# Two routed scatters: GpSimd's wait moved from every eighth transfer's own landing to every fourth, for the four before

## The reference, cut to what matters

```python
logits = flat.astype(jnp.float32) @ router_w.T + router_bias
scores = jax.nn.softmax(logits, axis=-1)
topk_scores, topk_idx = jax.lax.top_k(scores, TOPK)
topk_scores = topk_scores / jnp.clip(topk_scores.sum(axis=-1, keepdims=True), 1e-12, None)
h = jax.nn.silu(jnp.einsum('nd,ehd->neh', flat, gate_w)) * jnp.einsum('nd,ehd->neh', flat, up_w)
expert_out = jnp.einsum('neh,edh->ned', h, down_w)
sel = jnp.take_along_axis(expert_out, topk_idx[:, :, None], axis=1)
out = (sel * topk_scores.astype(flat.dtype)[:, :, None]).sum(axis=1)
out = out + jax.nn.silu(flat @ sgate_w.T) * (flat @ sup_w.T) @ sdown_w.T
```

## Time and profile before

| | |
|---|---|
| median of 3 runs | 1180.38 us (1178.22 to 1186.05) |
| profiled execution | 1180.22 us, of it a span of 1178.4 us |
| granted TensorE clock, mean | 0.837 of full speed |
| busy: PE, DVE, ACT, POOL | 859.4, 738.5, 660.3, 514.8 us |
| layer 0's routed stage | about 305 to 643 us |
| layer 1's routed stage | about 886 us to the end |

### The profile page before, as it was taken

One profiled execution on the slowest core, in us unless ns is written; L12 is line 12 of the kernel. 1 busy time (PEld: TensorE's weight loads), 2 busy tenths in 40 slices (PEclk: granted clock), 3 DMA queues, 4 the chain that ended last, 5 costly groups with the idle time before them and its releaser, 6 DMA issues. The chain is left out here.

```text
span 1178.4 us, 19964 instructions
## 1 busy us (share of the span) xinstructions
PE 859.4 (73%) x5812; PEld 698.0 (59%) x5812; DVE 738.5 (63%) x2343; ACT 660.3 (56%) x1352; POOL 514.8 (44%) x634
## 2 busy tenths in 40 slices
PE   3796666666156999995996546787676999999900
PEld 2633455555145888995995223444345989999900
DVE  5579588888765466410668599997986551004636
ACT  4354777777453324663664657677675656666600
POOL 0002555555206666666774777000002666125365
PEclk9998677777555999997998767788885999999965
DMA  7960000000511115655774111000004123233232
GB/s 207 290 195 0 1 0 0 0 0 1 222 34 43 46 43 159 188 165 154 192 195 128 48 45 48 0 1 1 1 1 165 42 90 105 86 84 102 60 91 60
DMA packets 133844, 97.00 MB, mean 82 GB/s; under 512 B 11648, under 2 KB 125696, under 8 KB 132736
## 3 DMA queue, kind: packets, MB, share of 16 engines
q1 hardware_dynamic: 121472, 70.79, 20.0%
q0 software_dynamic: 12288, 25.19, 7.3%
HBM read 45.61 MB, written 50.33 MB: 81 GB/s over the span
## 5 line engine op out<-in xcount | busy, mean ns | idle before, releaser
L1117 POOL DMA_INDIRECT e_xs<-h_tok,rows_of x128 | 129.3, 1010 | 101.2 <-DVEq L1600 35.4
L735 ACT ACTIVATE mask<-ps_q,k_neg 128x256 bf16<-128x256 f32 x256 | 101.0, 489 | 35.1 <-PE ps_q L850 35.1
L1130 POOL DMA_INDIRECT e_got<-e_ys,e_rows_of x64 | 65.9, 1030 | 93.7 <-DMA e_ys<-e_y_rows 67.9
L850 PE MATMUL ps_q<-q_parts,pick 128*128 (+1 forms) x256 | 59.1, 366 | 49.7 <-DVE mask L651 42.1
L1266 PE MATMUL e_ps_gu<-e_w_all,e_x_turned 128*128 x384 | 92.7, 385 | 0.5 <-ACT e_x_turned L1435 0.5
L1758 DVE TENSOR_TENSOR e_hidden<-e_ps_gu,e_hidden 128x512 f32<-128x512 f32 x48 | 33.2, 691 | 93.9 <-ACT e_hidden L1441 93.6
L1117 POOL DMA_INDIRECT e_xs<-h_tok,e_rows_of x64 | 65.5, 1023 | 51.3 <-DVEq L1600 19.2
L1298 PE MATMUL e_ps_up<-e_x_turned,e_w_up 128*128 128x128 f32 x640 | 84.5, 275 | 1.0 <-ACT e_x_turned L1435 1.0
L2253 POOL DMA_INDIRECT c_got<-e_ys,rows_of x64 | 71.1, 1111 | 31.3 <-issue 19.2
L1309 PE MATMUL e_ps_y<-e_w_all,e_hidden 128*128 x640 | 84.2, 275 | 0.0
L651 DVE TENSOR_TENSOR mask<-ps_q,k_tok 128x1024 bf16<-128x1024 f32 x64 | 75.2, 1216 | 10.2 <-PE ps_q L850 8.2
(11 more groups left out here) (399 smaller groups left out, 2430.9 us busy)
## 6 DMA issues: line engine op xcount, KB each, us to landing
e_x_rows<-e_xs SPq DMA_DIRECT2D x68, 256.0 KB, 2.9
e_ys<-e_y_rows SPq DMA_DIRECT2D x68, 256.0 KB, 2.5
e_xs<-zeros SPq DMA_DIRECT2D x2, 6144.0 KB, 34.2
e_w_all<-in_w SPq DMA_DIRECT2D x4, 1536.0 KB, 13.0
e_xs<-zeros SPq DMA_DIRECT2D x2, 2560.0 KB, 27.8
e_w_all<-in_w SPq DMA_DIRECT2D x4, 1024.0 KB, 10.2
x_tok<-in_x SPq DMA_DIRECT2D x4, 512.0 KB, 6.0
e_xs<-h_tok,rows_of POOLq DMA_INDIRECT x128, 2.3
```

Source lines behind the costliest of these rows:

```text
L735: last = nc.scalar.activation(mask[u][QS // 2 + j][keys][:, h * T:(h + 1) * T], psq[1][:, h * T:(h + 1) * T], ACT.Sign, bias=k_neg[u][:, k ...
L850: last = nc.tensor.matmul(psq[0 if on_dve else 1][:, h * T:(h + 1) * T], pick[:, (quad * HQ + h) * P:(quad * HQ + h + 1) * P], q_parts[:, ...
L1117: nc.gpsimd.indirect_dma_start(out=xs[part], out_offset=bass.IndirectOffsetOnAxis(ap=rows_of[:, t * K + k:t * K + k + 1], axis=0), in_=til ...
L1130: nc.gpsimd.indirect_dma_start(out=got[t % GB][:, k * P:(k + 1) * P], out_offset=None, in_=ys[part], in_offset=bass.IndirectOffsetOnAxis(a ...
```

## The change

The wait for landings moves back by four transfers and comes after every fourth. Each part has two semaphores in place of one for each group of four tiles; fours of transfers raise them in turn. After a four, GpSimd waits for the four before it, not for the one just issued. The last four of a part is waited for by SP's first load alone. SP waits for both semaphores of the part to reach their whole count. The same lines serve both layers.

```diff
-        scattered = [plain(f"scattered{i}") for i in range(GROUPS)]
+        CHUNK = 4
+        CHUNKS = PT * K // CHUNK
+        scattered = [[plain(f"scattered{part}_{i}") for i in range(2)] for part in range(NP)]
...
                     if q == 0:
-                        for g in range(part * GPP, (part + 1) * GPP):
-                            sp.wait_ge(scattered[g], 16 * TPG * K)
+                        for done in scattered[part]:
+                            sp.wait_ge(done, 16 * CHUNK * CHUNKS // 2)
...
                             nc.gpsimd.indirect_dma_start(
                                 out=xs[part], out_offset=bass.IndirectOffsetOnAxis(ap=rows_of[:, t * K + k:t * K + k + 1], axis=0),
-                                in_=tile(h_tok, t), in_offset=None, bounds_check=ROWS - 1).then_inc(scattered[t // TPG], 16)
-                        if (t + 1) * K % 8 == 0:
-                            pool.wait_ge(scattered[t // TPG], 16 * K * (t % TPG + 1))
+                                in_=tile(h_tok, t), in_offset=None,
+                                bounds_check=ROWS - 1).then_inc(scattered[part][(t - part * PT) * K // CHUNK % 2], 16)
+                        c, rest = divmod((t - part * PT + 1) * K, CHUNK)
+                        if rest == 0 and c >= 2:
+                            pool.wait_ge(scattered[part][c % 2], 16 * CHUNK * (c // 2))
```

## The result

| | before | after |
|---|---|---|
| median | 1180.88 us (1178.22 to 1186.05, 6 runs) | 1173.17 us (1170.36 to 1174.46, 6 runs) |
| profiled execution | 1180.22 us, span 1178.4 | 1170.36 us, span 1168.6 |

The ratio is 0.9926, with a 95% interval of 0.9908 to 0.9944: between 6.6 and 10.9 us less. The forecast of 1172.8 lies 0.4 us from the median. The profiled execution of after is the fastest of its six runs, so not all of its 9.8 us may be put down to the change; which part may is told behind the rows. One execution of an experiment's kernel ("layer 1 alone") was in a slow state, 1311.3 us at a granted clock of 0.688, and is left out of its median.

A forecast was written before the change was run, and what follows sets the result against it. The scatter was taken to bound only the seam between layer 0's halves. The gathers allowed 6.1 + 1.3 = 7.4 us, TensorE 8.2; the later end decides, layer 1 counts nothing: 1180.2 - 7.4 = 1172.8 us, range 1168.5 to 1178.0.

The forecast's parts named there:

- The drains and the waits: Layer 0's scatter: 16 drains removed, 30 waits cost nothing unless a landing passes 5.7 us; part 1 ends 18.8 us early.
- TensorE's path: Seam of layer 0's halves: load 24 follows the last store, so TensorE restarts at 541.7, 8.2 us sooner.
- no gain of clock: TensorE at the seam: the shorter stand still slows its clock; were it kept up, 2.4 us more.
- GpSimd's path: Layer 0: first gather waits for part 0's stores, starts 6.1 us sooner; with 1.3 slack, 7.4 us, which decides.
- The step took 3.3: Seam: from part 0's last store issued to the first gather, layer 1's 3.2 us plus 0.1.
- the 1.3 of slack: Layer 0's end: the last gathers landed 1.3 us before VectorE combined them; range 0.1 to 1.6.
- VectorE's wait of 0.8: Layer 0's end: VectorE waits some 0.8 us for the last gathers.
- The stages behind: After layer 0: everything between the layers moves as a whole; layer 1 loses 13.2 us of drains, costed at nothing.
- B: Layer 0: more slack in the gathers and TensorE keeps its clock, 10.6 us gained, 1169.6; chance 0.08.
- C: Scatter: transfers take longer on GpSimd without drains; gain gone at about 27 us more, 1180; chance 0.10.
- D: Scatter: undrained transfers pile up and land later, 14.2 us late at a landing of 8.0, 1194.4; chance 0.06.

The follow-up runs named there:

- layer 1 alone: Against the kernel before: new wait only in layer 1, layer 0 left instruction for instruction; 1180.70 us beside 1180.28, ratio 1.0002.
- one behind: Changed kernel with fours made ones: behind every transfer GpSimd waits for the one before it; 1201.88 us, ratio to before 1.0167.
- two behind: Changed kernel with fours made twos: behind every second transfer a wait for the two before; 1171.49 us, ratio to before 0.993.
- eight behind: Changed kernel with fours made eights: GpSimd waits for the eight before; 1173.61 us beside 1180.28, ratio to before 0.9942.
- drains on two semaphores: Changed kernel with the new wait in layer 1 only; layer 0 drains behind every eighth, each drain over two semaphores; 1183.86 us, ratio to before 1.0037.
- the changed kernel again: The changed kernel, nothing altered, measured once more beside other kernels; 1172.23 us, ratio to before 0.993.
- part 0 alone: Changed kernel with the new wait only in part 0 of layer 0, drains behind every eighth elsewhere; 1172.3 us, ratio to before 0.9938.

## Why the prediction was right

**The drains and the waits.** Forecast: waits behind four cost nothing, part 1 starts at 435.1 and its last transfer at 517.8. Found: 434.81 and 517.99, and every gap within a part 0.30 to 0.32. The kernels with one, two and eight behind confirm the step that the wait holds only where a landing passes its cover: in nearly every pair with one behind, at a few with two (where none was forecast), never with four or eight.

**TensorE's path.** Forecast: load 24 at 539.0, restart at 541.7, a stand of 3.9, no gain of clock. The times on the clock lie 1.3 to 1.8 earlier, since this execution's first turn did (450.99 against 452.75). Counted from that turn the restart is 7.8 us sooner, not 8.2. The load took 540.37 - 537.20 = 3.17 us to TensorE where 2.64 was taken over from before. The clock did fall, as assumed, but the row it was read from was weaker than it looked; more on that at the end.

**GpSimd's path** decides, as forecast, and here lies the term that was mis-sized. The last store was issued at 526.85 + 10.23 - 0.36 = 536.72 and the first gather started at 540.43, 3.71 later. The step took 3.3, from layer 1, where it was 3.20 before and is 3.20 after (1039.03 to 1042.23). The last store landed in 2.8 us at the seam, and in 2.3 in layer 1: the whole 0.5 by which this step is longer than layer 1's, and inside the 2.3 to 3.6 that the forecast allowed for. A stretch view of after shows what differs around it; first the seam, then layer 1 (length, busy time of the five engines, clock, DMA share, GB/s):

```profile
536.70:540.40 3.70, 0.03 (x1) 0.03 (x1) 0.00 (x0) 0.00 (x0) 0.00 (x0) 0.83 0.96 269
1039.00:1042.20 3.20, 3.20 (x31) 3.20 (x30) 0.00 (x0) 2.23 (x4) 0.00 (x0) 1.00 0.47 136
```

At the seam four loads are issued right behind the last store, and the DMA engines are busy 0.96 of the time, twice as much as in layer 1. The price taken from layer 1 had no loads on its heels. That the loads make the landing longer isn't shown, though. Where the scatter ends after that store, no load follows it. Two such traces have its landing: 2.3 us with the drains on two semaphores, and 3.0 with one behind. With loads right behind it, it landed in 2.7 in the kernel with two behind, in 2.8 in the changed kernel again, and in 3.3 with four loads moved ahead of it and two behind. Layer 1's landed in 2.3 in all ten traces. So the landing at the seam is longer and spreads; why stays open.

The rest of the path, counted from TensorE's first turn: the first gather came 5.74 us sooner (forecast 6.1), the last one 5.38 (the 64 took 83.40 us between the first and last start, 83.04 before), and it was combined 626.39 - 623.83 = 2.56 us after its start where 2.85 was reckoned. With the 1.3 of slack that is 5.38 + 1.3 + 0.29 = 7.0, against 6.9 measured and 7.4 forecast. The forecast's pace of the gathers was 0.36 too fast, the landing of the last ones 0.29 too long; the two nearly cancel. That 1172.8 lies as near the median as 0.4 us is in part luck: the seam's rows give 0.5 less than forecast, the medians 0.3 more. VectorE's wait of 0.8 was 0.97, and 2.4 in the changed kernel's second trace.

**The stages behind.** Layer 1 unchanged: 292.1 and 292.5 us, and the clean kernel's ratio of 1.0002. Everything between moved as a whole, but for the 1.5 us of the RWKV stage.

**The rivals.** B fell on both legs: the clock fell over the stand of 4.32 us, and where it was kept up by loading ahead the gathers held the end. C: GpSimd's 128 transfers took 129.6 us (129.3 before); nothing stretched. The Trainium skill's rule there (SBUF — State Buffer, Who interferes with whom: VectorE in some modes locks GpSimd out of the port when it issues first) had no visible effect here, though both halves of the scatter moved beside other VectorE work. D: no recorded landing of the scatters over 4.0 in after or with the wait eight behind, and no gap in layer 0 over 0.31, so in after no landing that was waited for passed 5.7. The margin was smaller than the forecast's 4.0 makes it: one behind has the gap of 4.29, which read as a landing is 5.8. The Trainium skill's 4.1 us at high load, an estimate by the page DMA: Bandwidth & Descriptors (Latency and other measured facts), is near the longest recorded landings (4.0 in after, 4.3 in "layer 1 alone"), but it isn't a bound if that gap is one.

**What the seam does not explain.** The medians say 7.7 with an interval of 6.6 to 10.9, the seam's rows 6.1 to 7.0 in the changed kernel (both traces) and in those with two, eight and part 0 alone. The difference lies inside the intervals; no run shows a second cause.

## What to carry to other kernels

Add up what a drain costs, then look at who waits for the drained engine: of 46.6 us of idle time at drains in two layers the kernel got back 7, because everything past the moment when part 0's own stores end was hidden already, and half of one layer's drains would have done. A wait that looks one batch back is free as soon as the transfers issued behind the one awaited cover its landing at the busiest moment, not at the median: four did here, two cost 5 us that happened to be hidden, and one cost the whole gain and 21 us more. And when a wait is removed, price its successor with its spread and not by one quiet row: the store that now comes last landed in 2.3 to 3.3 us at the seam, and in 2.3 each time in layer 1.

## What the runs showed of the hardware

**The same stand, with and without a fall of TensorE's clock.** The forecast's "no gain of clock" rested on a stand of 3.48 us that was followed by a slow turn. The trace of after has the same stand at the same place of the RWKV stage (133.9 us behind its first gather, 133.8 before), and the turn is quick:

```profile
769.33 0.66 PE L2269 MATMUL c_ps_t<-ident,y_tok 128*128 128x128 f32 x4 [3.48 <-ACT y_tok L2190]
```

The stretch behind it, before (first) and after (second), with the clock in the fourth column:

```profile
777.80:781.00 3.20, 3.16 (x7) 0.50 0.00 0
```

```profile
769.30:772.50 3.20, 3.17 (x11) 1.00 0.00 0
```

TensorE gets 11 products through in place of 7. The ten traces have 60 such stands of 3.48 us in that stage, six each, all from a granted clock of 1.00: 41 are followed by four turns in 1.0 to 1.1 us, 14 by 0.66, and five by 0.78 to 0.96. In the trace that the forecast could see, all six were slow. So the length of a stand alone doesn't say whether the clock falls from full speed, 2.4 GHz, to half. The nine stands of 4.25 us or more at the seam were all followed by a clock of 0.50 to 0.56 over the next 3 us (four turns in 1.11 us, but 0.91 in the changed kernel again and 0.83 with eight behind).

What a quick turn is worth to the stage isn't shown: with three quick ones of six it took 240.8 us in after, but 243.3 with two behind and 243.9 with eight, and with none 242.2 to 242.5. So the 1.5 us by which the stage was shorter in after stay open. The moment at which the clock rises in the shared branch does move one execution against another, by most of 1.8 us between the two traces, and a change of half a per cent is to be read against that.

**A drain over two semaphores** took 2.10 us at most places where one over a single semaphore took 2.03. The two layer-1 kernels differ only in how layer 0's scatter is waited for (the drains' two semaphores for one, SP's two for four), so the 4.6 us lie there. Half of the scatter's 3.5 is the drain beside the four stores; why the others got longer was not followed up.
